# Node update of a graph layer: VectorE's sums one unit further ahead, slice weights folded in the first units, residual in three pieces

## The chip, the cores and the metric

The kernel runs on 1 core of one Trainium2 chip. The metric is the device time of one execution in microseconds, the median of several runs.

## The reference

One layer over a graph of 6250 nodes (256 features each) and 100,000 edges. `xn` is the row-wise layer norm of `x`.

```
x = x + gnn(xn, edges) + mix(xn)          # gnn: messages, then the node update below
x = x + ffn(layernorm(x))                 # ffn: slice attention over 8 heads of 64 slices

# the node update, inside gnn
agg  = segment_sum(msg, dst, 6250)
h    = silu(agg @ Wu1 + bu1) @ Wu2 + bu2
bn   = gamma * (h - mean(h, axis=0)) * rsqrt(var(h, axis=0) + 1e-5) + beta
return xn + bn

# the start of ffn; x_mid is (x @ W_x + b_x), cut into 8 heads
slice_weights = softmax((x_mid @ W_slice + b_slice) / clip(temperature, 0.1, 5))
```

The mean and variance of `h` run over all nodes, so no node can be normalised before `h` of the last node exists. `W_x @ W_slice / temp` and its bias don't depend on the nodes: they can be multiplied into one matrix beforehand ("folded").

## The kernel before

The kernel is a row of stages, each a block in which every engine has a program of its own and in which engines meet only at semaphores: `opening`, `messages_and_attention` (most of the time), `update_nodes`, `slice_tokens`, `slice_attention`, `slice_output`. Every engine runs its own instructions strictly in the order written, so an instruction that waits holds up all behind it on its engine. The change is inside `update_nodes`.

**The units.** The nodes are 49 tiles of 128. `update_nodes` walks over them in 13 units: 2 tiles, then eleven units of 4 tiles, then 3. The aggregated messages come in as 4 partial tables in DRAM. For each unit u:

- SyncE (SP) loads the unit's rows of the four tables, 512 KB each for a unit of 4 tiles, into one of 4 buffer sets (`load`). Sets 0 and 1 are the tensors `part`; sets 2 and 3 are lent from `g.res`, rows of tiles 0 to 15 and 16 to 31, which are free until the residual is loaded. In the trace the tile is therefore called `part` or `res`. A set is loaded again once its unit has been summed (`agg_ready`) and transposed (`turned`).
- GpSimd (POOL) adds tables 2 and 3 (`late_sums`, line 1521). VectorE (DVE) adds tables 0 and 1 (line 1544), then GpSimd's sum (line 1547); both are `gather_sums`. Both operands of all these additions lie in SBUF.
- TensorE (PE) transposes the sum (`turn_sums`, line 1383), ScalarE (ACT) rounds it to `agg_high` (`high_sums`, line 1467), VectorE subtracts to get `agg_low` (`low_sums`, line 1553, one operand in PSUM).
- TensorE multiplies by Wu1 in three high/low products (`hidden`, line 1395, 12 matmuls). ScalarE applies silu (line 1474) and rounds (line 1481), GpSimd subtracts (`low_hidden`, line 1526, both operands in SBUF). TensorE multiplies by Wu2 (`nodes`, line 1409, 12 matmuls), ScalarE copies out to `hT` (`copy_h`, line 1486), VectorE takes the statistics (`node_stats`, line 1558, one operand).

TensorE's order is `hidden(u)`, `turn_sums(u+1)`, `nodes(u-1)`. ScalarE's is silu and round of u, `high_sums(u+1)`, `copy_h(u-1)`. GpSimd's is `low_hidden(u)`, `late_sums(u+2)`. VectorE's is

```
for u in range(UNITS):
    if u + 1 < UNITS:
        gather_sums(u + 1)
        low_sums(u + 1)
    if u:
        for f in range(CB):
            node_stats(u - 1, f)
```

so that on VectorE `node_stats(u-1)` stands between `low_sums(u+1)` and `gather_sums(u+2)`.

**The end of the stage.** After the last unit VectorE joins the statistics (line 1611), ScalarE takes the square root (line 1504), and VectorE runs `fold_slices` (lines 1564 to 1582), for which TensorE has multiplied the slice weights (lines 1428, 1431, 1435) after its last `nodes`. Only then come the reciprocal (line 1616) and three small operations that give scale and shift. Then the back part: ScalarE normalises `hT` unit by unit (line 1509), TensorE transposes it back (line 1445), VectorE adds the residual (line 1629) and takes row statistics (line 1633). The residual is loaded in two pieces (lines 1371 and 1372) once the last unit is summed and transposed, since half of the lent sets is in use until then.

Of the kernel before, what the change touches and what calls it, by code (L numbers as in the profile page):

```python
# [43 lines left out]
TABLES = 4  # L44
# [1207 lines left out]
SETS = 4  # L1252

# [17 lines left out]
def update_nodes(nc, sem, sb, g):  # L1271
# [61 lines left out]
    FOLD_BIAS = 7  # L1333
    heads = lambda ap: ap.rearrange("p (h n) -> p h n", h=FH)
# [17 lines left out]
    with nc.Block() as block:  # L1352
        @block.sync
        def _(sp):
# [13 lines left out]
            sp.wait_ge(agg_ready, UNITS)  # L1368
            sp.wait_ge(turned, PAIRS_BEFORE[UNITS])
            half = NT // 2  # L1370
            sp.dma_start(g.res[:, 0:half, :], split_rows(g.res_dram, 0, half)).then_inc(res_in, 16)
            sp.dma_start(g.res[:, half:NT, :], split_rows(g.res_dram, half, NT - half)).then_inc(res_in, 16)

        @block.tensor
        def _(pe):
# [36 lines left out]

            turn_sums(0)
# [10 lines left out]
            pe.wait_ge(turn_low, PAIRS_BEFORE[UNITS])  # L1424
            pe.wait_ge(hid_ready, CB * UNITS)
            for b in range(CB):
                for h in range(FH):
                    nc.tensor.matmul(g.ps[b][:, ds(h * FG, FG)], wx_t[:, h, ds(b * P, P)], w_slice[:],
                                     start=True, stop=True)
            for h in range(FH):  # L1430
                mm = nc.tensor.matmul(g.ps[2][0:1, ds(h * FG, FG)], b_x[:, h:h + 1], w_slice[:], start=True, stop=True)
            mm.then_inc(folded, 1)

            pe.wait_ge(fold, FOLD_BIAS)
            nc.tensor.matmul(g.ps[3][0:BIAS_ROWS, :], ends[:], bias[:], start=True, stop=True).then_inc(folded, 1)

# [78 lines left out]
        def _(pool):  # L1515
# [13 lines left out]
            late_sums(0)  # L1529
            late_sums(1)  # L1530
            for u in range(UNITS):
                for f in range(CB):
                    low_hidden(u, f)
                if u + 2 < UNITS:
                    late_sums(u + 2)

        @block.vector
        def _(dve):
# [21 lines left out]
            def fold_slices():  # L1560

                dve.wait_ge(fold, 5)
                dve.wait_ge(folded, 1)
                V.tensor_tensor(heads(bias[:]), heads(g.ps[2][0:1, :]),
                                b_slice[:].unsqueeze(1).to_broadcast([1, FH, FG]), ALU.add).then_inc(fold, 1)
                dve.wait_ge(fold, 6)
                V.tensor_tensor(heads(bias[:]), heads(bias[:]), wide(inv_temp[0:1, :], 1),
                                ALU.mult).then_inc(fold, 1)
                for b in range(CB):
                    V.tensor_tensor(heads(w_logit[:, b, :]), heads(g.ps[b][:]), wide(inv_temp[:], P),  # L1570
                                    ALU.mult).then_inc(logit_w, 1)
                dve.wait_ge(logit_w, CB)
# [3 lines left out]
                dve.wait_ge(folded, 2)  # L1576
                V.tensor_copy(spread, g.ps[3][0:BIAS_ROWS, :]).then_inc(fold, 1)
                dve.wait_ge(fold, 8)
                V.tensor_copy(g.logit_bias[:], spread).then_inc(fold, 1)
                dve.wait_ge(fold, 9)  # L1580
# [615 lines left out]
```

## Time and profile before

| | us |
|---|---|
| median of 3 runs | 2219.74 |
| lowest, highest run | 2217.71, 2225.6 |
| the profiled execution: its own time | 2217.5 |
| the profiled execution: span of its instructions | 2215.7 |
| `update_nodes` within it, first load to last row statistic | 1703.1 to 1876.8 |

Times are microseconds from the start of the span unless marked ns. In the rows DVE is VectorE, ACT ScalarE, POOL GpSimd, SP SyncE, PE TensorE's matmuls and PEld its weight loads. L1544 is line 1544 of the kernel. A row of the timeline gives start, duration, engine, line, operation, output and inputs, and in brackets how long the engine had been idle before and which instruction ended that. In the table of windows the columns are the stretch, its length, for PE, PEld, DVE, ACT and POOL the busy time with the count of instructions, then PEclk, the DMA share and GB/s. PEclk is the mean clock that TensorE was granted, 1.00 for 2.4 GHz and 0.50 for 1.2 GHz; DMA is the mean busy share of the DMA engines.

### The profile page before, as it was taken

To read this page: it belongs to the slowest core of one execution; us is meant where nothing else is said; L and a number is where in the kernel's file an instruction comes from. 1 tells how busy PE (TensorE), PEld (TensorE's weight loads), DVE (VectorE), ACT (ScalarE), POOL (GpSimd) and SP (SyncE) were. 2 spreads that over 40 slices of the span, in tenths; PEclk is the share of its full clock that TensorE was granted. 3 is DMA by queue.
4 is the path that set the end of the run, shared out by engine and by line. 5 is a ranking of instruction groups with operands and counts; after the bars stand their busy time and mean duration, and the time that the engine had idled before them with its cause. 6 is when DMAs were issued, how large, how long until landed. Compare 5 with 4: busy or idle time off the path is not lost. (4 is left out here: it accounts for less than half of the span.)

```text
span 2215.7 us, 38972 instructions
## 1 busy us (share of the span) xinstructions
PE 1914.7 (86%) x10218; PEld 1580.6 (71%) x10218; DVE 1531.5 (69%) x3525; ACT 1306.3 (59%) x2330; POOL 1437.9 (65%) x989
## 2 busy tenths in 40 slices
PE   3687999999889988998899989998990785999878
PEld 2466788777777777877787777877880574788678
DVE  6654777777767767776777676767771568999645
ACT  2333776776676657765776676667660463666423
POOL 2121888888888888888888888888885550455300
PEclk9898999999999999999999999999995895999979
DMA  8756888988888889878888888898886951000002
GB/s 280 278 223 204 159 156 153 188 152 147 146 179 156 152 156 172 156 138 161 168 156 155 176 154 156 142 181 156 148 132 112 329 161 54 1 0 0 20 20 97
DMA packets 288441, 325.45 MB, mean 147 GB/s; under 512 B 29575, under 2 KB 251178, under 8 KB 288146
## 3 DMA queue, kind: packets, MB, share of 16 engines
q0 software_dynamic: 112896, 102.81, 37.8%
q1 hardware_dynamic: 169568, 216.13, 30.8%
q10 hardware_dynamic: 5746, 3.90, 0.7%
q8 instruction: 88, 1.44, 0.3%
q14 instruction: 143, 1.17, 0.2%
HBM read 167.64 MB, written 154.97 MB: 146 GB/s over the span
## 5 line engine op out<-in xcount | busy, mean ns | idle before, releaser
L903 POOL DMA_INDIRECT sums<-summed,out_idx x784 | 1236.1, 1577 | 295.1 <-issue 209.5
L957 PE MATMUL bank<-wf,hidT 128*128 128x256 f32 x3136 | 798.3, 383 | 0.0
L957 PEld LDWEIGHTS bank<-wf,hidT 128*128 128x128 f32 x3136 | 544.5, 192 | 54.1
L1048 ACT ACTIVATE hidT<-bank,bf 128x512 f32<-128x512 f32 x392 | 269.8, 688 | 263.0 <-PE bank L935 216.6
L1143 DVE TENSOR_TENSOR msg_low<-msg,msg_high 128x512 fp32r<-128x512 f32 x392 | 272.4, 695 | 180.0 <-ACT msg_high L1068 133.5
L1174 DVE TENSOR_TENSOR msg<-bank,gathered 128x512 f32<-128x512 f32 x392 | 269.4, 687 | 111.3 <-PE bank L957 83.5
L1068 ACT ACTIVATE msg_high<-msg 128x512 fp32r<-128x512 f32 x392 | 247.2, 631 | 93.2 <-DVE msg L1174 83.6
L955 PE MATMUL bank<-gnn_bf_halves,ones 128*128 128x256 f32 x784 | 297.1, 379 | 0.0
L1056 ACT ACTIVATE summed<-pair 128x516 f32<-128x516 f32 x392 | 230.2, 587 | 59.2 <-DMA sums<-summed,out_idx 56.1
L1075 ACT ACTIVATE gathered<-bank 128x512 f32<-128x512 f32 x392 | 231.9, 592 | 51.0 <-issue 22.6
L945 PE MATMUL bank<-window,spread 128*128 128x256 f32 x784 | 194.1, 329 | 66.7 <-DVE spread L1138 38.9
L935 PE MATMUL bank<-attr_parts,wf_parts 128*128 128x512 f32 x392 | 224.4, 572 | 26.2 <-DVE attr_parts L1128 22.5
L969 PE MATMUL pair<-msg_high,same 128*128 128x258 f32 x784 | 209.3, 288 | 21.8 <-ACT summed L1056 14.4
L945 PEld LDWEIGHTS bank<-window,spread 128*128 128x128 f32 x784 | 124.6, 191 | 129.5 <-issue 86.1
L969 PE MATMUL pair<-msg_low,same 128*128 128x258 f32 x784 | 206.3, 284 | 0.0
L1138 DVE TENSOR_TENSOR spread<-id_row,half_f 128x256 fp32r<-128x256 uint8 x392 | 165.4, 422 | 26.5 <-issue 17.6
L969 PEld LDWEIGHTS pair<-msg_high,same 128*128 128x128 f32 x784 | 149.5, 191 | 45.2 <-issue 21.0
L1153 DVE TENSOR_TENSOR same<-id_row,src_f 128x256 fp32r<-128x256 int16 x392 | 162.7, 416 | 0.0
L969 PEld LDWEIGHTS pair<-msg_low,same 128*128 128x128 f32 x784 | 148.8, 190 | 15.3
L955 PEld LDWEIGHTS bank<-gnn_bf_halves,ones 128*128 128x128 f32 x784 | 150.2, 192 | 10.7
L1163 DVE SCALAR_TENSOR_TENSOR redirect<-summed,first_limit,to_trash 128x2 f32<-128x2 f32 x392 | 85.5, 218 | 57.7 <-ACT summed L1056 45.7
L935 PEld LDWEIGHTS bank<-attr_parts,wf_parts 128*128 128x128 f32 x392 | 75.2, 192 | 63.3 <-issue 38.5
(329 smaller groups left out, 2818.6 us busy)
## 6 DMA issues: line engine op xcount, KB each, us to landing
window<-xn_halves SPq DMA_DIRECT2D x392, 128.0 KB
sums<-gate SPq DMA_DIRECT2D x32, 800.0 KB, 10.0
id_row<-id_rows SPq DMA_DIRECT2D x98, 256.0 KB
attr<-attr_rows SPq DMA_DIRECT2D x98, 256.0 KB
xn_halves<-xn_halves SPq DMA_DIRECT2D x7, 1792.0 KB, 6.6
id_row<-id_rows SPq DMA_DIRECT2D x98, 128.0 KB
sums<-summed,out_idx POOLq DMA_INDIRECT x784
res<-sums SPq DMA_DIRECT2D x24, 512.0 KB, 8.4
```

Of the source, the lines that this page charges most:

```text
L903: nc.gpsimd.indirect_dma_start(g.sums_dram[k], bass.IndirectOffsetOnAxis(ap=out_idx[:, ET * c + t:ET * c + t + 1], axis=0), summed[c % 2][ ...
L935: T.matmul(hps[:], g.wf1_parts[:, h, ds(f * P, P)], attr_parts[:, p, :], start=True, stop=True).then_inc(hid_made, 1)
L945: mm = T.matmul(gps[:, ds(t * C, C)], spread[:, j % 2, ds(t * P, P)], window[:, j, :], start=True, stop=True)
L955: T.matmul(out, g.ones2[:], g.bf2[:], start=True, stop=False)
L957: mm = T.matmul(out, hidT[:, j // 2, f, ds((2 * (j % 2) + t) * P, P)], g.wf2[:, f, :], start=False, stop=f == CB - 1)
L969: mm = T.matmul(sps[:, t, 0:XW], same[:, p, 2 * j + t, :], half[:, j % 2, t, :], start=k == 0, stop=k == 1)
L1048: A.activation(hidT[:, h, f, :], hps[:], ACT.Silu, bias=g.bf1[:, f:f + 1]).then_inc(hid_ready, 1)
L1056: A.activation(summed[p][:, ds(2 * j, 2), :], sps[:, :, 0:XW], ACT.Copy).then_inc(sum_ready, 1)
L1068: A.activation(msg_high[:, j % 2, :, 0:C], msg[:, j % 2, :, :], ACT.Copy).then_inc(high_ready, 1)
L1075: A.activation(gathered[:, j, :, :], gps[:].rearrange("p (t c) -> p t c", c=C), ACT.Copy).then_inc(gath_copied, 1)
L1143: V.tensor_tensor(msg_low[:, j % 2, :, 0:C], msg[:, j % 2, :, :], msg_high[:, j % 2, :, 0:C].bitcast(F32), ALU.subtract).then_inc(low_read ...
L1174: V.tensor_tensor(msg[:, j % 2, :, :], fps[j % 2][:].rearrange("p (t c) -> p t c", c=C), gathered[:, j, :, :], ALU.mult).then_inc(msg_read ...
```

## The change

Four edits, all in `update_nodes`.

1. On VectorE `gather_sums` runs one unit further ahead, and before `node_stats`. Its order is now `low_sums(u+1)`, `gather_sums(u+2)`, `node_stats(u-1)`.
2. GpSimd's `late_sums` runs 3 units ahead instead of 2.
3. The fold of the slice weights moves from the end to the first units. TensorE runs `fold_weights` after `hidden(0)` and `fold_ends` in unit 2; VectorE runs `fold_bias` before unit 1's `low_sums`, `fold_logits`, `round_logits` and `spread_bias` in units 0, 1 and 2. Banks 5 to 7 and the last columns of `hT`, unused that early, hold the intermediate results.
4. The residual comes in three pieces: tiles 32 to 48 behind the last table load, tiles 0 to 15 once unit 10 has been summed and transposed, tiles 16 to 31 once unit 11 has.

```diff
+AHEAD = 3
-    flat = [part[p][:, 0, :, :].rearrange("p t c -> p (t c)") for p in range(2)]
-    w_logit = flat[0].rearrange("p (b n) -> p b n", b=CB)
-    spread = flat[1][0:BIAS_ROWS, 0:HG]
+    w_logit = hT[:, :, ds(NPAD - HG, HG)]
+    spread = hT[0:BIAS_ROWS, 0, ds(NPAD - 2 * HG, HG)]
+    FOLDED_BANKS, BIAS_BANK, ENDS_BANK = g.ps[6:8], g.ps[5], g.ps[6]
+    LENT_SETS = {2: 0, 3: 1}
+    LENT = len(LENT_SETS) * TABLES * UT
+    LENT_SPLIT = TABLES * UT
...
         def _(sp):
...
-            sp.wait_ge(agg_ready, UNITS)
-            sp.wait_ge(turned, PAIRS_BEFORE[UNITS])
-            half = NT // 2
-            sp.dma_start(g.res[:, 0:half, :], split_rows(g.res_dram, 0, half)).then_inc(res_in, 16)
-            sp.dma_start(g.res[:, half:NT, :], split_rows(g.res_dram, half, NT - half)).then_inc(res_in, 16)
+            sp.dma_start(g.res[:, LENT:NT, :], split_rows(g.res_dram, LENT, NT - LENT)).then_inc(res_in, 16)
+            for u, landed in ((UNITS - 3, res_in), (UNITS - 2, slice_in)):
+                at = LENT_SETS[u % SETS] * TABLES * UT
+                sp.wait_ge(agg_ready, u + 1)
+                sp.wait_ge(turned, PAIRS_BEFORE[u + 1])
+                sp.dma_start(g.res[:, at:at + TABLES * UT, :], split_rows(g.res_dram, at, TABLES * UT))\
+                  .then_inc(landed, 16)
...
         def _(pe):
...
             def nodes(u):
...
+                if u == 0:
+                    pe.wait_ge(fold, FOLD_BIAS - 1)
...
             for u in range(UNITS):
                 hidden(u)
+                if u == 0:
+                    fold_weights()
                 if u + 1 < UNITS:
                     turn_sums(u + 1)
+                if u == 2:
+                    fold_ends()
                 if u:
                     nodes(u - 1)
             nodes(UNITS - 1)
-            pe.wait_ge(slice_in, 80)
...
-            mm.then_inc(folded, 1)
-
-            pe.wait_ge(fold, FOLD_BIAS)
...
+            pe.wait_ge(fold, FOLD_STEPS)
...
         def _(pool):
...
-            late_sums(0)
-            late_sums(1)
+            for u in range(AHEAD):
+                late_sums(u)
             for u in range(UNITS):
                 for f in range(CB):
                     low_hidden(u, f)
-                if u + 2 < UNITS:
-                    late_sums(u + 2)
+                if u + AHEAD < UNITS:
+                    late_sums(u + AHEAD)
...
         def _(dve):
...
+            gather_sums(1)
+            fold_bias()
             for u in range(UNITS):
                 if u + 1 < UNITS:
-                    gather_sums(u + 1)
                     low_sums(u + 1)
+                if u + 2 < UNITS:
+                    gather_sums(u + 2)
+                if u == 0:
+                    fold_logits()
+                if u == 1:
+                    round_logits()
+                if u == 2:
+                    spread_bias()
                 if u:
                     for f in range(CB):
                         node_stats(u - 1, f)
...
             V.tensor_scalar(sd[:], mv[:, :, 1], EPS, None, ALU.add).then_inc(chain, 1)
-            fold_slices()
             dve.wait_ge(chain, 4)
...
                     dve.wait_ge(back_made, n + 1)
+                    if LENT_SPLIT in tiles:
+                        dve.wait_ge(slice_in, 96)
```

`fold_weights` holds the matmuls of lines 1431 and 1428, in that order, `fold_ends` that of line 1435. `fold_bias`, `fold_logits`, `round_logits` and `spread_bias` hold the instructions of `fold_slices`, lines 1564 to 1582, in their old order.

## Rows read from the trace of the kernel before

**Rows 1.** Busy time by windows: units 1-3, units 4-11, end chain, back part.

```profile
1731.38:1757.92 26.54, 22.15 (x96) 17.80 (x97) 15.27 (x17) 13.18 (x23) 13.64 (x9) 0.86 1.10 348
1757.92:1819.17 61.25, 52.39 (x255) 41.83 (x254) 39.41 (x49) 38.72 (x64) 37.62 (x24) 1.00 0.52 164
...
1828.70:1840.76 12.06, 5.61 (x35) 3.37 (x34) 6.87 (x15) 2.57 (x5) 0.00 (x0) 0.60 0.70 225
1840.76:1876.80 36.04, 21.93 (x94) 15.42 (x94) 34.72 (x82) 15.68 (x24) 0.00 (x0) 0.59 0.00 0
```

**Rows 2.** Timeline of TensorE, one unit: hidden, transposes, nodes, next hidden.

```profile
1796.66 0.39 PE L1395 MATMUL bank<-agg_high,wu1h 128*128 128x512 f32 x1
...
1800.72 1.09 PE L1383 MATMUL bank<-ident,res 128*128 128x128 f32 x8 [1.17 <-DVE res L1547]
1801.57 0.48 PE L1409 MATMUL pair<-hid_high,wu2h 128*128 128x512 f32 x1
...
1804.42 0.39 PE L1395 MATMUL bank<-agg_high,wu1h 128*128 128x512 f32 x1
```

**Rows 3.** Timeline of VectorE, the same unit and the next sums.

```profile
1802.10 1.29 DVE L1553 TENSOR_TENSOR agg_low<-bank,agg_high 128x512 fp32r<-128x512 f32 x2 [1.44 <-ACT agg_high L1467]
...
1805.35 0.69 DVE L1558 BATCH_NORM_STATS2 bn_raw<-hT 128x6 f32<-128x512 f32 x1 [0.69 <-ACT hT L1486]
1805.96 1.21 DVE L1544 TENSOR_TENSOR res<-res 128x1024 f32<-128x1024 f32 x1
1807.20 1.23 DVE L1547 TENSOR_TENSOR res<-res 128x1024 f32<-128x1024 f32 x1
```

**Rows 4.** Timeline of ScalarE, the same unit.

```profile
1801.47 1.09 ACT L1467 ACTIVATE agg_high<-bank 128x512 fp32r<-128x512 f32 x2 [0.16 <-PE bank L1383]
...
1804.62 0.69 ACT L1486 ACTIVATE hT<-pair,bu 128x512 f32<-128x512 f32 x1 [0.69 <-PE pair L1409]
```

**Rows 5.** Timeline of GpSimd, unit 2's sum, and the same unit as above.

```profile
1728.83 2.35 POOL L1521 TENSOR_TENSOR res<-res 128x1024 f32<-128x1024 f32 x1 [0.30 <-DMA res<-sums]
...
1800.87 2.53 POOL L1526 TENSOR_TENSOR hid_low<-hidT_u,hid_high 128x512 fp32r<-128x512 f32 x2 [2.84 <-ACT hid_high L1481]
1803.36 2.39 POOL L1521 TENSOR_TENSOR res<-res 128x1024 f32<-128x1024 f32 x1
```

**Rows 6.** Timeline, unit 3: a sum on GpSimd and one on VectorE meet.

```profile
1740.11 2.40 POOL L1521 TENSOR_TENSOR res<-res 128x1024 f32<-128x1024 f32 x1
1740.46 3.13 DVE L1544 TENSOR_TENSOR res<-res 128x1024 f32<-128x1024 f32 x1
```

**Rows 7.** Timeline, the end chain: fold matmuls, root, reciprocal, first residual add.

```profile
1826.36 3.78 PE L1428 MATMUL bank<-w_slice,wx_t 64*128 64x64 f32 x32
...
1828.76 0.20 ACT L1504 ACTIVATE bn_sd<-bn_sd 128x2 f32<-128x2 f32 x1 [0.42 <-DVE bn_sd L1613]
1830.07 1.05 PE L1431 MATMUL bank<-w_slice,b_x 64*1 64x64 f32 x16
...
1832.68 2.07 PE L1435 MATMUL bank<-slice_bias,slice_bias_ends 1*128 1x512 f32 x2 [1.56 <-DVE slice_bias L1567]
...
1837.60 0.17 DVE L1616 RECIPROCAL bn_sd<-bn_sd 128x2 f32<-128x2 f32 x1
...
1840.76 0.69 DVE L1629 TENSOR_TENSOR res<-pair,res 128x512 f32<-128x512 f32 x1 [2.40 <-PE pair L1445]
```

**Rows 8.** The DMA issue of the residual's second half, on SP's timeline.

```profile
1817.09 5.10 SPq L1372 DMA_DIRECT2D res<-res_rows  x1
```

**Rows 9.** DMA issues by size: the last number is us from issue to landing.

```profile
res<-res_rows SPq DMA_DIRECT2D x1, 3200.0 KB, 21.2
```

**Rows 10.** Timeline, the opening: slice weights landed, and unit 1's first transposes.

```profile
1720.92 0.17 DVE L1597 TENSOR_SCALAR temp<-temp 128x8 f32<-128x8 f32 x1 [2.35 <-DMA temp<-w_ffn_temperature]
...
1728.00 1.97 PE L1383 MATMUL bank<-ident,part 128*128 128x128 f32 x8 [6.38 <-DVE part L1547]
```

**Rows 11.** Busy time by windows: just behind unit 0's hidden.

```profile
1721.70:1725.50 3.80, 0.00 (x0) 0.00 (x0) 1.23 (x1) 1.04 (x3) 2.70 (x1) 0.95 1.10 349
```

More of the change, by code:

```diff
@@ L1411, in nodes, with fold_weights, fold_ends @@
                     mm.then_inc(h_made, 1)
+            def fold_weights():
+                pe.wait_ge(slice_in, 80)
+                for h in range(FH):
+                    mm = nc.tensor.matmul(BIAS_BANK[0:1, ds(h * FG, FG)], b_x[:, h:h + 1], w_slice[:],
+                                          start=True, stop=True)
+                mm.then_inc(folded, 1)
+                for b in range(CB):
+                    for h in range(FH):
+                        mm = nc.tensor.matmul(FOLDED_BANKS[b][:, ds(h * FG, FG)], wx_t[:, h, ds(b * P, P)],
+                                              w_slice[:], start=True, stop=True)
+                mm.then_inc(folded, 1)
+            def fold_ends():
+                pe.wait_ge(fold, FOLD_BIAS)
+                pe.wait_ge(logit_w, CB)
+                nc.tensor.matmul(ENDS_BANK[0:BIAS_ROWS, :], ends[:], bias[:], start=True, stop=True)\
+                  .then_inc(folded, 1)
             turn_sums(0)
@@ L1421, in _ @@
             nodes(UNITS - 1)
-            pe.wait_ge(slice_in, 80)
[L1424 to L1431, printed above, removed]
-            mm.then_inc(folded, 1)
-            pe.wait_ge(fold, FOLD_BIAS)
-            nc.tensor.matmul(g.ps[3][0:BIAS_ROWS, :], ends[:], bias[:], start=True, stop=True).then_inc(folded, 1)
+            pe.wait_ge(fold, FOLD_STEPS)
             for u in range(UNITS):
@@ L1558, in node_stats, with fold_bias, fold_logits, round_logits @@
                 V.bn_stats(raw[:, f, u, :], hT[:, f, ds(UNIT_AT[u] * P, unit_nodes(u))]).then_inc(stats, 1)
[L1560 removed]
+            def fold_bias():
                 dve.wait_ge(fold, 5)
                 dve.wait_ge(folded, 1)
[L1564 removed]
+                V.tensor_tensor(heads(bias[:]), heads(BIAS_BANK[0:1, :]),
                                 b_slice[:].unsqueeze(1).to_broadcast([1, FH, FG]), ALU.add).then_inc(fold, 1)
[L1566 removed]
+                dve.wait_ge(fold, FOLD_BIAS - 1)
                 V.tensor_tensor(heads(bias[:]), heads(bias[:]), wide(inv_temp[0:1, :], 1),
                                 ALU.mult).then_inc(fold, 1)
+            def fold_logits():
+                dve.wait_ge(folded, 2)
                 for b in range(CB):
[L1570 removed]
+                    V.tensor_tensor(heads(w_logit[:, b, :]), heads(FOLDED_BANKS[b][:]), wide(inv_temp[:], P),
                                     ALU.mult).then_inc(logit_w, 1)
+            def round_logits():
                 dve.wait_ge(logit_w, CB)
@@ L1575, in fold_slices, with spread_bias @@
                 V.tensor_tensor(g.logit_low[:], w_logit, g.logit_high[:].bitcast(F32), ALU.subtract)
-                dve.wait_ge(folded, 2)
-                V.tensor_copy(spread, g.ps[3][0:BIAS_ROWS, :]).then_inc(fold, 1)
-                dve.wait_ge(fold, 8)
+            def spread_bias():
+                dve.wait_ge(folded, 3)
+                V.tensor_copy(spread, ENDS_BANK[0:BIAS_ROWS, :]).then_inc(fold, 1)
+                dve.wait_ge(fold, FOLD_BIAS + 1)
                 V.tensor_copy(g.logit_bias[:], spread).then_inc(fold, 1)
-                dve.wait_ge(fold, 9)
+                dve.wait_ge(fold, FOLD_STEPS)
                 low = slice(LOW_ROW, LOW_ROW + 1)
```

1 line of the change is left out of this document (added).

## The prediction

> **What bounds the kernel now.** I read the table of windows first, to see what each stretch of the stage is worth and who fills it, then the timelines of the engines over one unit, and last the timeline of the end. `update_nodes` is 174 us of the run and falls into four stretches [rows 1]. From `hidden(1)` to `hidden(4)` 26.54 us pass, with a granted clock of 0.86: part of it ran at 1.2 GHz. From `hidden(4)` to `hidden(12)` it is 61.25 us for eight units, 7.66 each, at full clock. Then an end chain, 12.06 us from the square root to the first residual add, in which TensorE and GpSimd are nearly idle. Then the back part, 36.04 us, in which VectorE is busy for 34.72: nothing of the change touches its work, so it only moves.
>
> In a full unit 7.76 us lie between two `hidden` (1796.66 to 1804.42) [rows 2]. TensorE is not the bound: it stands idle 1.17 us ahead of its transposes, for the sum. Followed back, the wait is a ring: transposes 0.85 (1800.72 to 1801.57) [rows 2], `nodes` 2.85 (1801.57 to 1804.42), then 0.20 until ScalarE's copy starts, 0.69 for the copy (from 1804.62) [rows 4], 0.65 until the statistics on it are out of VectorE's way (1805.31 to 1805.96) [rows 3], the two sums 2.47 (1805.96 to 1808.43) [rows 3], 0.05 to the next transposes. That adds to 7.76, the whole period. The statistics need `nodes`, the sums behind them don't; only VectorE's order ties them.
>
> **The end chain.** The root is ready at 1828.76 + 0.20 = 1828.96 and the reciprocal that needs it starts at 1837.60 [rows 7]. Between lie the fold's instructions: VectorE waits for the matmuls (3.78 and 1.05 us), then does its nine. Without them the reciprocal starts some 0.1 us behind the root, as the other steps of that chain follow each other. That removes 8.5 us, and the first residual add comes at 1832.3 instead of 1840.76.
>
> It needs the residual to be there. Before, the second half was issued at 1817.09 [rows 8] and landed 21.2 us later [rows 9], at 1838.3: left so, it would have given back 6.0 of the 8.5. Edit 4 removes that: the last piece waits only for the transposes of unit 11, some 15 us ahead of the end of the loop, and is 2 MB; at the 348 GB/s that the DMA engines moved when full [rows 1] it takes 6 us. The first piece joins SP's queue behind all table loads, so it delays none. Edit 4 costs nothing then, as long as the loop still covers it.
>
> **The steady units.** With the sums of u+2 issued ahead of the statistics the ring above is cut. What is late next? Three things stand close together. TensorE itself: 7.76 less the 1.17 of idling, 6.59 us. The chain that needs one `hidden` for the next: from `hidden` at 1796.66 through silu and rounding to the end of `agg_low` at 1803.39 [rows 3], less the 0.16 for which ScalarE waited for transposes [rows 4], 6.57. And the side-by-side work of VectorE and GpSimd.
>
> That third one is why I don't take 6.6. In unit 3 a sum on VectorE started at 1740.46 while one on GpSimd ran from 1740.11 to 1742.51; it lasted 3.13 us, against 1.21 alone, and ended 1.08 after GpSimd's did [rows 6, 3]. So these operations, with both operands in SBUF, exclude each other. `agg_low` with an operand in PSUM, and the statistics with one operand, overlap GpSimd's work without growing. Per unit GpSimd holds 2.53 + 2.39 = 4.92 [rows 5], VectorE 1.21 + 1.23 = 2.44: together 7.36. At present they hardly meet, because the sums start at 1805.96, just behind GpSimd's end at 1805.75. Moved ahead of the statistics, they start about where `late_sums` does, and the two collide in every unit. A handover hides a little (1.08 of 1.21), four of them at about 0.15 take 7.36 to 6.8. So the period has its bounds at 6.6 (no cost of collision) and 7.76 (all gain lost to it). I take 7.1 for full units: above 6.8, because the lock is idle while GpSimd waits for the rounding, and below 7.36, because VectorE's other 2.7 us of work don't need it. On eight units, the last one shorter, I count 0.62 each, 5.0 us; bounds 0 and 8 x 1.06 = 8.5.
>
> The Trainium skill ("SBUF — State Buffer", section Who interferes with whom) says that a VectorE instruction with two SBUF inputs contends with a GpSimd instruction that reads SBUF, and that whoever issues first holds the port for the whole instruction. The row of unit 3 agrees, 3.13 us for 1.21. By that rule taken strictly the period would not fall under the 7.36 of the plain sum, and the eight units would give 2.4 us instead of 5.0.
>
> **The first units.** From `hidden(1)` to `hidden(4)` three units take 26.54 us, 3.3 more than three steady ones: low clock, and the blocked sum of 3.13. At the new period three units are 21.3. Against it stands what the fold adds there: on TensorE one matmul of 2.07 us, measured at 1.2 GHz [rows 7], about half of it if the clock is up; on VectorE 3.7 us of rounding and spreading in units 1 and 2, ahead of the next `agg_low`, and VectorE was busy only 15.27 of 26.54 [rows 1]. I let 1.0 us of both reach the path: 22.3, a gain of 4.2. Bounds: 0, if the clock stays low, and 6.7, if the period is 6.6 and the fold is hidden.
>
> **The opening.** The matmuls of `fold_weights` fall behind `hidden(0)`, which ends at 1721.7; the slice weights had landed at 1720.9, and TensorE then idled 6.38 us to 1728.00 [rows 10]. They take 3.78 + 1.05 = 4.8 us at full clock, and the stretch behind `hidden(0)` was granted 0.95 [rows 11]: done at 1726.5, at no cost. At 1.2 GHz I bound them at twice that, 9.7, less the 6.38 of cover: 3.3 late. `fold_bias` on VectorE, 1.4 us, follows unit 1's sum and ends as `agg_high` of unit 1 does. The third `late_sums` on GpSimd, now ahead of `low_hidden(0)`, needs unit 2, which landed at 1728.8 [rows 5]; it ends at 1731.2, `low_hidden(0)` some 2.4 later, and `nodes(0)`, behind `hidden(1)`, asks for it only at about 1735. A unit's tables are 2.1 MB, 6.0 us at 348 GB/s: unit 3 at 1734.8, unit 4 at 1740.8, and so on. Sums at a period of 7.1 fall further behind these landings with each unit, so the DMA is not the bound, though by just 1.1 us a unit.
>
> **The sum.** 8.5 + 4.2 + 5.0 = 17.7 us. The profiled execution took 2217.5 us, the median of the runs is 2219.74, 2.2 above it and the lowest run 2217.71; I take the middle, 2218.6, and get 2200.9, as 2201.
>
> **The rivals.**
>
> *Collision eats the loop.* The idle wait for the sum goes, but VectorE blocked behind `late_sums` brings `agg_low` late instead; the period stays at 7.66 and the opening gives 2.0. Then 8.5 + 2.0 = 10.5: 2208. For it: the row of 3.13 and the 7.36. Against: VectorE waits 1.44 us ahead of `agg_low` at present [rows 3] and has room for one blocked sum.
>
> *TensorE-bound.* The engines fall into a phase in which they don't meet: period 6.6, 8.5 + 6.7 + 8.5 = 23.7, 2195. Against: the lock would have to be busy without a gap.
>
> *The opening pays back.* The fold's matmuls run at 1.2 GHz and `hidden(1)` is 3.3 late: 14.4 us, 2204. For it: the clock was at 0.50 again when the transposes came; against: the 0.95 just before.
>
> *Slower.* VectorE loses the lock ahead of each of its two sums, once to `late_sums` and once to both `low_hidden`: its own round is 1.29 + 2.39 + 1.21 + 2.53 + 1.23 + 1.38 = 10.0 us. Eight units then lose 18.7, the first three 3.5, the end gives 8.5: 13.7 slower, 2232. It decides from a period of about 9. Against it: in unit 3 VectorE got the lock as soon as the running GpSimd instruction ended.
>
> **Chances.** Forecast 0.50, collision 0.20, TensorE-bound 0.13, opening 0.14, slower 0.03. The range takes the two ends of the steady and first units: 2194 (all at 6.6, and the median at the lower side) to 2209 (the collision case). 0.5% of 2219.74 is 11.1 us, so faster is below 2208.6, about what a measurement of this kernel can tell from no change. Of the collision case 0.12 falls below and 0.08 within, and of the opening's 0.01 within: faster 0.88, same 0.09, slower 0.03.
>
> **What would show it.** The reciprocal directly behind the root, and the first residual add, with no wait for a DMA, some 3.4 us behind the root. No idle time of TensorE ahead of the transposes; in its place a small wait for `agg_low`. Means of lines 1544, 1547, 1521 and 1526 that grow, by a few tenths of a us and up to 2: the sum of the growths is the price of the collision. A period near 7.1. A period of 7.6 or more, a `hidden(1)` later than 1732, or a residual add that waits for its piece would each make the prediction wrong.

## The result, and the profile after

| | before | changed |
|---|---|---|
| median, us | 2220.25 (7 runs) | 2211.66 (7 runs) |
| lowest to highest | 2217.71 to 2225.6 | 2209.71 to 2215.68 |
| the profiled execution, own time / span | 2217.5 / 2215.7 | 2210.18 / 2208.4 |

The ratio is 0.9959, with a 95% interval from 0.9947 to 0.9972: faster, by 8.6 us, where 17.7 had been forecast. The measured time lies above the stated range.

The message stage ahead of `update_nodes` ends some microseconds earlier or later in each execution: in the profiles of this study `update_nodes` begins between 1702 and 1712 us. So the stage is read by itself here. This table holds the stretches of `update_nodes`, taken from the timelines of ScalarE and VectorE. S is VectorE's first instruction in the stage, s1, s4 and s12 are ScalarE's first silu of units 1, 4 and 12, A is the joining of the statistics, R the first residual add, E the start of the last reciprocal.

| execution | S to s1 | s1 to s4 | s4 to s12 | s12 to A | A to R | R to E | stage |
|---|---|---|---|---|---|---|---|
| before | 31.15 | 25.13 | 60.96 | 7.21 | 13.11 | 35.53 | 173.1 |
| before, again | 30.14 | 24.62 | 60.86 | 7.23 | 13.56 | 35.54 | 172.0 |
| changed | 30.50 | 26.91 | 58.52 | 7.24 | 4.56 | 35.53 | 163.3 |
| changed, again | 34.37 | 26.85 | 58.50 | 7.24 | 4.56 | 35.54 | 167.1 |

The end gives 8.55 to 9.0 us, as forecast. Units 4 to 11 give 2.4 instead of 5.0, the first units lose 1.8 to 2.2 instead of giving 4.2, and the opening is as before in one execution and 3 to 4 us longer in the other. Part of that last difference is no work of the change: the first silu of unit 0 comes 17.18 and 16.17 us after S in the two executions of before, 16.30 and 18.05 in the two of the changed kernel. Counted from that silu, the stage takes 155.9 and 155.8 us before, 147.0 and 149.0 changed.

The table of windows of the changed kernel, for the stretches of [rows 1]; the first two again go from `hidden(1)` to `hidden(4)` and on to `hidden(12)`:

```profile
1732.42:1760.60 28.18, 25.20 (x98) 18.98 (x98) 22.81 (x24) 12.97 (x23) 19.63 (x12) 0.79 1.10 348
1760.60:1819.45 58.85, 52.41 (x255) 41.83 (x255) 53.38 (x49) 38.19 (x64) 41.09 (x24) 1.00 0.82 266
1829.10:1832.62 3.52, 1.08 (x4) 0.71 (x4) 0.69 (x6) 2.63 (x6) 0.00 (x0) 0.54 0.00 0
1832.62:1868.65 36.03, 22.06 (x94) 15.52 (x94) 34.73 (x82) 15.62 (x24) 0.00 (x0) 0.59 0.00 0
```

In the second row VectorE is busy for 53.38 us against 39.41 before, with the same 49 instructions, and GpSimd for 41.09 against 37.62. Nothing was added there: the 14 and 3.5 us are time in which an instruction had begun and stood still. In the first row the clock is 0.79 instead of 0.86.

VectorE's timeline over one steady unit of the changed kernel (lines 1571, 1562, 1565 and 1576 are what 1553, 1544, 1547 and 1558 were), answering to [rows 3]:

```profile
1789.09 1.29 DVE L1571 TENSOR_TENSOR agg_low<-bank,agg_high 128x512 fp32r<-128x512 f32 x2 [0.35 <-ACT agg_high L1485]
1790.29 1.46 DVE L1562 TENSOR_TENSOR part<-part 128x1024 f32<-128x1024 f32 x1
1791.79 3.30 DVE L1565 TENSOR_TENSOR part<-part 128x1024 f32<-128x1024 f32 x1
1795.02 1.27 DVE L1576 BATCH_NORM_STATS2 bn_raw<-hT 128x6 f32<-128x512 f32 x2
1796.53 1.29 DVE L1571 TENSOR_TENSOR agg_low<-bank,agg_high 128x512 fp32r<-128x512 f32 x2 [0.24 <-ACT agg_high L1485]
```

and GpSimd's beside it, answering to [rows 5]:

```profile
1788.12 2.55 POOL L1544 TENSOR_TENSOR hid_low<-hidT_u,hid_high 128x512 fp32r<-128x512 f32 x2 [2.93 <-ACT hid_high L1499]
1790.63 3.38 POOL L1539 TENSOR_TENSOR res<-res 128x1024 f32<-128x1024 f32 x1
```

VectorE's second sum starts at 1791.79 and lasts 3.30 us instead of 1.23: GpSimd's sum, from 1790.63 to 1794.01, has the port. (It lasts 3.38 instead of 2.39 because VectorE's first sum had it until about 1791.7.) VectorE now goes from one `agg_low` to the next with hardly any idle time, 7.44 us: its own blocked work is the period. In some units it is the first sum that is blocked, behind GpSimd's sum, and the second that is free:

```profile
1782.81 3.47 DVE L1562 TENSOR_TENSOR part<-part 128x1024 f32<-128x1024 f32 x1
1786.31 1.23 DVE L1565 TENSOR_TENSOR part<-part 128x1024 f32<-128x1024 f32 x1
```

The period is therefore not one number. From silu to silu units 4 to 11 take 8.25, 7.11, 7.82, 7.36, 7.55, 7.37, 7.00 and 6.06 us, and in the second execution the same to 0.05; the first seven have a mean of 7.49. Where the text says 7.4, it means the shown unit.

The end, VectorE's timeline, answering to [rows 7]:

```profile
1829.40 0.17 DVE L1648 RECIPROCAL bn_sd<-bn_sd 128x2 f32<-128x2 f32 x1 [0.27 <-ACT bn_sd L1522]
...
1832.62 0.69 DVE L1663 TENSOR_TENSOR res<-pair,res 128x512 f32<-128x512 f32 x1 [2.46 <-PE pair L1463]
```

The reciprocal waits for the root alone, the residual add for transposes alone.

TensorE's timeline in units 1 and 2 (line 1437 is the bias matmul, formerly 1435):

```profile
1745.96 1.09 PE L1390 MATMUL bank<-ident,res 128*128 128x128 f32 x8 [1.63 <-DVE res L1565]
1746.98 1.62 PE L1437 MATMUL bank<-slice_bias,slice_bias_ends 1*128 1x512 f32 x2
1748.53 0.80 PE L1418 MATMUL pair<-hid_high,wu2h 128*128 128x512 f32 x1
1749.13 0.63 PE L1418 MATMUL pair<-hid_low,wu2h 128*128 128x512 f32 x1
```

and VectorE's:

```profile
1742.61 3.29 DVE L1565 TENSOR_TENSOR res<-res 128x1024 f32<-128x1024 f32 x1
1745.83 1.76 DVE L1595 CAST logit_high<-hT 128x1024 fp32r<-128x1024 f32 x1
1747.62 2.17 DVE L1597 TENSOR_TENSOR logit_low<-hT,logit_high 128x1024 fp32r<-128x1024 f32 x1
```

In the kernel before, the two instructions of the rounding stood in the end chain, with no GpSimd instruction beside them:

```profile
1833.86 0.70 DVE L1573 CAST logit_high<-part 128x1024 fp32r<-128x1024 f32 x1
1834.59 1.22 DVE L1575 TENSOR_TENSOR logit_low<-part,logit_high 128x1024 fp32r<-128x1024 f32 x1
```

Unit 3's sum is blocked to 3.29 us, TensorE idles 1.63 us for it, does 1.55 us of fold ahead of `nodes(1)`, and then runs `nodes(1)` with 0.63 us per matmul, at 1.2 GHz (0.39 at 2.4).

### The profile page after: what moved, and what is told of

Read it like the earlier page. It is cut to its first block and busy times, and to the rows that moved or that the text cites. A ratio compares the mean times of both kernels' runs of the same rounds, so it can differ in the third digit from the quotient of the medians.

```text
span 2208.4 us, 38977 instructions
## 1 busy us (share of the span) xinstructions
PE 1923.6 (87%) x10218; PEld 1586.1 (72%) x10218; DVE 1548.5 (70%) x3525; ACT 1306.1 (59%) x2330; POOL 1447.2 (66%) x989
## 5 line engine op out<-in xcount | busy, mean ns | idle before, releaser
L969 PEld LDWEIGHTS pair<-msg_high,same 128*128 128x128 f32 x784 | 149.7, 191 | 41.6 <-issue 16.4
```

The lines of the kernel that those rows point to most:

```text
L969: mm = T.matmul(sps[:, t, 0:XW], same[:, p, 2 * j + t, :], half[:, j % 2, t, :], start=k == 0, stop=k == 1)
```

## The experiments

Each ratio is to the kernel before, run on the same chip. The stage times stand in one table behind the experiments.

**E1. Fold and residual alone.**

```diff
-AHEAD = 3
+AHEAD = 2
...
             for u in range(UNITS):
                 if u + 1 < UNITS:
+                    if u:
+                        gather_sums(u + 1)
                     low_sums(u + 1)
-                if u + 2 < UNITS:
-                    gather_sums(u + 2)
```

> Edits 3 and 4 alone (fold in the first units, residual in three pieces); the order of the sums on VectorE and GpSimd is that of before. Theory P (collision): VectorE's sums moved ahead of the statistics collide with GpSimd's sums and give nearly nothing net, so the two other edits carry the whole gain: end chain 8.5 us shorter, units 4 to 11 at the old period of 7.75, first three units up to 1.5 us longer for the fold's work on VectorE and TensorE; in all 7 to 8.5 us faster than before, ratio 0.9962 to 0.9968. Theory F (the fold costs the gain): the fold's instructions in units 1 and 2 are what lengthened the first units by 1.8 us and more; then this kernel is only 4 to 6 us faster, ratio 0.9973 to 0.9982.

Ratio 1.0006 (0.9991 to 1.002): no gain at all, though the end is 8.6 us shorter. Both expectations missed, theory F by less. It is all lost before unit 4: S to s1 takes 33.92, s1 to s4 32.09. TensorE's timeline:

```profile
1754.52 1.97 PE L1390 MATMUL bank<-ident,res 128*128 128x128 f32 x8 [5.92 <-DVE res L1565]
1756.42 2.07 PE L1437 MATMUL bank<-slice_bias,slice_bias_ends 1*128 1x512 f32 x2
```

and VectorE's ahead of it:

```profile
1745.44 0.90 DVE L1595 CAST logit_high<-hT 128x1024 fp32r<-128x1024 f32 x1
1746.37 3.31 DVE L1597 TENSOR_TENSOR logit_low<-hT,logit_high 128x1024 fp32r<-128x1024 f32 x1
```

In this order the rounding of the logits stands ahead of unit 3's sum. GpSimd blocks it (3.31 us for 1.22), TensorE idles 5.92 us, and runs the bias matmul and most of `nodes(1)` at 1.2 GHz. One unit takes 17.06 us. From unit 4 on the period is 7.74, as before.

**E2. The sums alone.**

```diff
-            late_sums(0)
-            late_sums(1)
+            for u in range(3):
+                late_sums(u)
...
-                if u + 2 < UNITS:
-                    late_sums(u + 2)
+                if u + 3 < UNITS:
+                    late_sums(u + 3)
...
+            gather_sums(1)
             for u in range(UNITS):
                 if u + 1 < UNITS:
-                    gather_sums(u + 1)
                     low_sums(u + 1)
+                if u + 2 < UNITS:
+                    gather_sums(u + 2)
```

> Edits 1 and 2 alone (VectorE's and GpSimd's sums one unit further ahead); fold and residual stay at the end. Theory P (collision): VectorE's second sum takes about 3.3 us in most units, the period is 7.5 instead of 7.75, 2 us over units 4 to 11, and the first units gain 0 to 2: 2 to 4 us faster, ratio 0.9982 to 0.9991. Theory F: without the fold in the way the edit gives what the prediction said of it, 9 us, ratio 0.996, with a period near 7.1.

Ratio 0.9973 (0.9953 to 0.9994), about 6 us; the stage is 167.2, shorter by 5 to 6. Units 4 to 11 give 3.3 to 3.4, the first units 0.4 to 0.9, the opening 0.6 to 1.6. From silu 1 to silu 12 the sums give 3.7 to 4.3 us, where the prediction's terms without the fold would be 10.2 (5.0, and 26.54 less 21.3). That is more than in the changed kernel, whose first units lose. The second sum is blocked to 3.3 us here too, as theory P had it, though the ratio lies between the two theories. The first units have a slow one here as well, without any fold: unit 3 takes 10.54 us, with TensorE idle for 2.35 us ahead of its transposes and the first matmuls of `nodes(2)` at 0.63 us each, so at 1.2 GHz.

**E3. GpSimd's sums left out.** VectorE adds table 2 alone and table 3 is not added, so the output isn't the reference's.

```diff
-            for u in range(AHEAD):
-                late_sums(u)
...
-                if u + AHEAD < UNITS:
-                    late_sums(u + AHEAD)
...
-                dve.wait_ge(late_ready, u + 1)
```

> The changed kernel with GpSimd's sums of tables 2 and 3 left out (VectorE adds table 2 alone, table 3 is not added), and the wait for them. Everything else as in the changed kernel, so GpSimd holds only 2.5 us per unit. Theory P: VectorE's sums take 1.2 us each again and the period falls to 6.6 to 6.8, TensorE or the chain through the rounding being the bound; 6 to 9 us faster than the changed kernel, ratio to before 0.992 to 0.9935. Rival D (the table loads, 6 us a unit, or the chain of VectorE's own work set the period): the period stays at 7.3 or more and the time within 2 us of the changed kernel.

Ratio 0.9925 (0.9902 to 0.9947). From unit 4 to unit 10 the period is 6.64 to 6.68, and s1 to s4 takes 21.42: theory P. TensorE has no idle time ahead of its transposes in these units. The table loads, which are unchanged, allow 6.65.

**E4. The residual loaded late.**

```diff
-            sp.dma_start(g.res[:, LENT:NT, :], split_rows(g.res_dram, LENT, NT - LENT)).then_inc(res_in, 16)
...
+            sp.wait_ge(agg_ready, UNITS)
+            sp.wait_ge(turned, PAIRS_BEFORE[UNITS])
+            half = NT // 2
+            sp.dma_start(g.res[:, 0:half, :], split_rows(g.res_dram, 0, half)).then_inc(res_in, 16)
+            sp.dma_start(g.res[:, half:NT, :], split_rows(g.res_dram, half, NT - half)).then_inc(res_in, 16)
...
-                    if LENT_SPLIT in tiles:
-                        dve.wait_ge(slice_in, 96)
```

> The changed kernel with the residual loaded as before, in two halves once the last unit is summed and transposed. If edit 4 carries most of the gain at the end: the first residual add waits for the second half, which lands about 21 us after its issue, 5 to 6 us later than in the changed kernel; ratio to before 0.998 to 0.999. If the residual is hidden anyway: within 1 us of the changed kernel, ratio 0.996.

Ratio 0.9992 (0.9977 to 1.0008). A to R takes 9.96 instead of 4.56, so edit 4 is worth 5.4 us, as the first of the two expectations had it. VectorE's timeline and the DMA issues:

```profile
1848.56 0.69 DVE L1659 TENSOR_TENSOR res<-pair,res 128x512 f32<-128x512 f32 x1 [7.87 <-DMA res<-res_rows]
```

```profile
res<-res_rows SPq DMA_DIRECT2D x1, 3200.0 KB, 20.7
```

**E5. The statistics between the two sums.**

```diff
                 if u + 2 < UNITS:
-                    gather_sums(u + 2)
+                    first_sum(u + 2)
...
                 if u:
                     for f in range(CB):
                         node_stats(u - 1, f)
+                if u + 2 < UNITS:
+                    second_sum(u + 2)
```

> The changed kernel with VectorE's statistics of u-1 put between its two sums of u+2 (first sum, both statistics, second sum); in units 0 to 2 the fold's instructions follow the second sum. If VectorE's blocked second sum sets the period (theory P): the 1.4 us of statistics now run while GpSimd holds the port, the period falls from 7.4 to 6.7 to 6.9, 4 to 6 us less on units 4 to 11; the stage 158 to 160 us against 163 to 166 of the changed kernel, ratio to before 0.993 to 0.995. If the sum of all exclusive work (4.92 + 2.44 = 7.36) is the bound whatever the order: period 7.3 or more, time as the changed kernel.

Ratio 0.9978 (0.9962 to 0.9994), period 8.15: worse than the old order. The first expectation missed; the second's "7.3 or more" is met in number only, since 8.15 is 0.8 above the sum of 7.36 that it went by. VectorE's timeline:

```profile
1791.95 3.19 DVE L1562 TENSOR_TENSOR part<-part 128x1024 f32<-128x1024 f32 x1
1795.06 1.27 DVE L1583 BATCH_NORM_STATS2 bn_raw<-hT 128x6 f32<-128x512 f32 x2
1796.26 1.20 DVE L1568 TENSOR_TENSOR part<-part 128x1024 f32<-128x1024 f32 x1
1798.90 1.29 DVE L1578 TENSOR_TENSOR agg_low<-bank,agg_high 128x512 fp32r<-128x512 f32 x2 [1.44 <-ACT agg_high L1485]
```

Now the first sum is the blocked one, and the statistics stand again ahead of something that the next transposes wait for. I had counted VectorE's round, 6 us, and forgotten the ring of the prediction: `agg_low`, blocked sum, statistics, second sum, transposes, rounding, `agg_low`, 8.16 in all.

**E6. VectorE's fold late.** TensorE's fold matmuls stay behind `hidden(0)`. VectorE's product and rounding move to its idle time in units 10 and 11, the spreading of the bias to the wait for the first back transposes.

```diff
-    w_logit = hT[:, :, ds(NPAD - HG, HG)]
-    spread = hT[0:BIAS_ROWS, 0, ds(NPAD - 2 * HG, HG)]
-    FOLDED_BANKS, BIAS_BANK, ENDS_BANK = g.ps[6:8], g.ps[5], g.ps[6]
+    flat = [part[1][:, k, :, :].rearrange("p t c -> p (t c)") for k in range(2)]
+    w_logit = flat[0].rearrange("p (b n) -> p b n", b=CB)
+    spread = flat[1][0:BIAS_ROWS, 0:HG]
+    FOLDED_BANKS, BIAS_BANK, ENDS_BANK = g.ps[6:8], g.ps[5], g.ps[2]
...
-                if u == 2:
-                    fold_ends()
...
             nodes(UNITS - 1)
+            fold_ends()
...
-                if u == 0:
-                    fold_logits()
-                if u == 1:
-                    round_logits()
-                if u == 2:
-                    spread_bias()
...
+                if u == UNITS - 3:
+                    fold_logits()
+                    high_logits()
+                if u == UNITS - 2:
+                    low_logits()
...
+            spread_bias()
             dve.wait_ge(res_in, 32)
```

> The changed kernel with VectorE's fold instructions taken out of units 0 to 2: product and rounding in VectorE's idle time of units 10 and 11, the bias's spreading while the first back transposes run, TensorE's bias matmul behind its last nodes. TensorE's other fold matmuls stay behind hidden(0). Theory F (VectorE's fold work in units 1 and 2 delays the next sum and lets TensorE idle and its clock fall): hidden(1) to hidden(4) falls from 26.9 to 24 or 25 us, as with the sums alone (24.2), the rest is unchanged, ratio to before 0.9945 to 0.9955. Rival: the 26.9 come from the collision of the sums and the low clock alone; then 26 to 27 and no change.

Ratio 0.9948 (0.9934 to 0.9961). s1 to s4 falls to 21.02, further than theory F had it, and, not expected, the later units fall too, to 54.65. The program of a steady unit is the changed kernel's, word for word; only the moment at which the engines come into it differs. VectorE's and GpSimd's timelines:

```profile
1790.86 1.30 DVE L1562 TENSOR_TENSOR res<-res 128x1024 f32<-128x1024 f32 x1
1792.20 2.20 DVE L1565 TENSOR_TENSOR res<-res 128x1024 f32<-128x1024 f32 x1
1794.32 1.27 DVE L1576 BATCH_NORM_STATS2 bn_raw<-hT 128x6 f32<-128x512 f32 x2
```

```profile
1789.79 3.52 POOL L1544 TENSOR_TENSOR hid_low<-hidT_u,hid_high 128x512 fp32r<-128x512 f32 x2
1793.27 3.37 POOL L1539 TENSOR_TENSOR res<-res 128x1024 f32<-128x1024 f32 x1
```

Here VectorE's first sum falls between the two instructions of `low_hidden`, and its second behind the second of them, ahead of GpSimd's whole sum. So it waits for an instruction of 1.25 us, not for one of 2.4: 2.20 instead of 3.30. GpSimd's two rows add to 6.89 us in a period of 6.82 (a row begins before the one ahead of it has quite ended): it has no gap. This execution was the fastest of its kernel's ten (2203.66, median 2209.19), so its stage of 152.2 overstates the usual gain. The timed intervals of E6 and of the changed kernel (0.9947 to 0.9972) overlap; the difference between the two is read from the profiles.

**E7. The fold's matmuls split.**

```diff
-                for b in range(CB):
-                    for h in range(FH):
+                fold_block(0)
...
+                if u == 1:
+                    fold_block(1)
...
-                if u == 0:
-                    fold_logits()
                 if u == 1:
+                    fold_logits()
                     round_logits()
```

> The changed kernel with the fold's matmuls split: the bias and the first half behind hidden(0), the second half behind nodes(0), and VectorE's product in unit 1 instead of unit 0. Theory O (at 1.2 GHz the matmuls take 8.8 us and outlast the 6.3 us gap behind hidden(0)): from the stage's start to the first silu of unit 1 it is 31 to 31.5 us in runs with the low clock, as in before, instead of 33.7; units 1 to 4 take 0.5 to 3 us more because VectorE has the whole fold in units 1 and 2. Rival: the delay is the wait for the slice weights' landing, and stays 33.7.

Ratio 0.9958 (0.9941 to 0.9974), as the changed kernel. S to s1 takes 30.14, but this execution had the higher clock there, so it doesn't tell the two apart (E8 does); s1 to s4 is 27.86, 1.0 longer.

**E8. E5, E6 and E7 together.**

> All three of these at once: statistics between the sums, VectorE's fold late, TensorE's fold matmuls split. If the three costs are separate, they add: opening 31.3, units 1 to 4 22 to 24, units 4 to 12 53 to 55, to the aggregate 7.2, to the first residual add 4.6, back part 35.5: stage 154 to 157 us against 173.1 of before, ratio to before 0.991 to 0.993, faster than the changed kernel by 6 to 10 us. If one bound lies behind another (the table loads at 6.0 us a unit above all): 160 or more.

Ratio 0.9962 (0.9942 to 0.9983), stage 158.2, units 4 to 12 in 58.00. They don't add: units 4 to 12 take 3.4 us more than in E6. The order of E5 is the likely reason; it wasn't taken out by itself.

This execution had the low clock in the opening, and so it settles E7's question. TensorE's timeline, the first half of the split matmuls:

```profile
1724.24 3.67 PE L1433 MATMUL bank<-w_slice,wx_t 64*128 64x64 f32 x16
```

Half of the matmuls take about half of the 7.08 us that all take at 1.2 GHz, and silu 0 to silu 1 is 14.06 us instead of 16.3: theory O. It is the length of the matmuls that delays unit 1, not the landing of the slice weights.

**E9. GpSimd's sums in halves.**

```diff
-                G.tensor_tensor(c, c, d, ALU.add).then_inc(late_ready, 1)
+                n = len(unit_tiles(u)) // 2
+                for a in (slice(0, n), slice(n, None)):
+                    G.tensor_tensor(c[:, a, :], c[:, a, :], d[:, a, :], ALU.add).then_inc(late_ready, 1)
...
-                dve.wait_ge(late_ready, u + 1)
+                dve.wait_ge(late_ready, 2 * (u + 1))
```

> The changed kernel with each of GpSimd's sums of tables 2 and 3 cut into two instructions of half the size; the same work, the same order. Theory G (VectorE is held up by the length of the one GpSimd instruction that runs when it asks, 2.4 us for a whole sum and 1.25 for a half or for one half of low_hidden; not by the total of the work): VectorE's second sum takes 2.2 us instead of 3.3, the period of units 4 to 11 falls from 7.4 to 6.8 or 6.9, units 4 to 12 take 54 to 56 us instead of 58.5; the stage 159 to 162 us, ratio to before 0.994 to 0.995. Rival S (the sum of all exclusive work, which is the same or a little more here, sets the period): 7.3 or more and 58 to 59 us.

Ratio 0.9937 (0.9912 to 0.9962). Units 4 to 12 take 54.64, the period is 6.95 to 7.15 in units 4 to 9, with the same work and order as the changed kernel: theory G. The timed intervals of the two overlap (four runs here); the gain of 3.9 us in these units is read from the profiles. VectorE's and GpSimd's timelines:

```profile
1791.29 1.60 DVE L1564 TENSOR_TENSOR part<-part 128x1024 f32<-128x1024 f32 x1
1792.92 2.19 DVE L1567 TENSOR_TENSOR part<-part 128x1024 f32<-128x1024 f32 x1
```

```profile
1791.77 4.49 POOL L1541 TENSOR_TENSOR part<-part 128x512 f32<-128x512 f32 x2
```

The first units are no better (28.04).

**E10. E6 and E9 together.**

> The kernel with VectorE's fold late (52.2 us less than 58.5 was not its aim, but its units 4 to 12 took 54.65) and in addition GpSimd's sums in halves. If the two are the same gain got twice over, the port being busy without a gap at 6.8 us a unit: units 4 to 12 54 to 55 us, stage 152 to 154, ratio 0.9935 to 0.995, no faster than with the late fold alone. If halves shorten the waits beyond that: period 6.65, 53 us, stage 150 to 151.

Ratio 0.9913 (0.9891 to 0.9935), the lowest of all, 19 us faster than before. Its units 4 to 12 take 55.23, no less than in E6 or E9 alone: the same gain, reached by two ways. It enters the steady units at another moment than E9 does (21.48 against 28.04 us from s1 to s4) and comes to the same period, 6.94 to 6.99 in units 4 to 9. So that period goes with the halved sums and not with a lucky entry, which could not be said from E9 alone.

The late fold has a price that E6 didn't show by itself: unit 11 takes 6.83 us from silu to silu here, and 6.85 in E6, against 6.04 in E9. VectorE's timeline of this kernel,

```profile
1810.37 1.71 DVE L1598 CAST logit_high<-part 128x1024 fp32r<-128x1024 f32 x1
1811.99 1.01 DVE L1573 TENSOR_TENSOR agg_low<-bank,agg_high 128x512 fp32r<-128x512 f32 x2
```

and of E9:

```profile
1824.59 1.02 DVE L1573 TENSOR_TENSOR agg_low<-bank,agg_high 128x512 fp32r<-128x512 f32 x2 [2.05 <-ACT agg_high L1485]
```

In E9 VectorE stands idle for 2.05 us and waits for ScalarE; here the cast, blocked to 1.71 us, keeps it until after ScalarE is ready, and `agg_low` of unit 12 is late by some 0.8 us.

Against E6 the intervals just touch, so whether the halves add anything to the late fold is open; against the changed kernel (0.9947 to 0.9972) it is faster.

**E11 and E12. The changed kernel and the one before, once more.**

> The changed kernel once more, for its stage times in another execution. Units 4 to 12 58.5 us again (the same pattern of collisions, which then is set by the program and not by chance); from the stage's start to the first silu of unit 1 either 30.5 us (fold matmuls at 2.4 GHz for most of it) or 33.7 (at 1.2 GHz).

> The kernel before once more. If the stage's time is a property of the program: 173 us from start to end of update_nodes, within 2 us, whatever the time of the whole run, whose spread of 10 us would then come from the message stage ahead of it.

2214.23 and 2222.13 us. The stretches stand at the top: those behind silu 1 repeat to 0.5 us, and from unit 2 on each single unit repeats to 0.1. The opening differs. TensorE's timeline of the changed kernel in its first execution:

```profile
1722.60 1.50 PE L1425 MATMUL pair<-w_slice,b_x 64*1 64x64 f32 x16 [0.17 <-DMA temp<-w_ffn_temperature]
1724.03 4.43 PE L1430 MATMUL bank<-w_slice,wx_t 64*128 64x64 f32 x32
1729.04 1.97 PE L1390 MATMUL bank<-ident,part 128*128 128x128 f32 x8 [0.58 <-DVE part L1565]
```

and in the second:

```profile
1722.81 1.86 PE L1425 MATMUL pair<-w_slice,b_x 64*1 64x64 f32 x16
1724.60 7.08 PE L1430 MATMUL bank<-w_slice,wx_t 64*128 64x64 f32 x32
1731.61 1.97 PE L1390 MATMUL bank<-ident,part 128*128 128x128 f32 x8
```

with the window that holds the second's matmuls:

```profile
1722.50:1731.60 9.10, 9.10 (x50) 8.55 (x49) 3.72 (x4) 1.08 (x3) 5.67 (x2) 0.50 1.10 349
```

At 1.2 GHz the fold takes 8.8 us and outlasts the gap of some 6.3; silu 0 to silu 1 then takes 16.32 instead of 14.20; the other 1.75 us by which this opening is longer lie ahead of silu 0. There VectorE's cast of Wu1, which waits for the small weights' loads, starts 11.68 us after S in the first execution and 13.43 in the second:

```profile
1716.57 0.43 DVE L1616 CAST wu1h<-wu 128x512 fp32r<-128x512 f32 x1 [0.65 <-DMA beta<-w_gnn_beta]
1717.01 0.43 DVE L1616 CAST wu1h<-wu 128x512 fp32r<-128x512 f32 x1 [2.13 <-DMA beta<-w_gnn_beta]
```

The two executions of before differ by 1.0 us in the same place. Of the nine profiles with the fold whole behind `hidden(0)`, six show the long opening (16.3 to 16.4 us from silu 0 to silu 1) and three the short one (13.7 to 14.4).

The stretches of the experiments; s12 to A takes 7.2 us in all of them, R to E 35.5 to 35.6:

| kernel | S to s1 | s1 to s4 | s4 to s12 | A to R | stage | ratio |
|---|---|---|---|---|---|---|
| E1 fold and residual alone | 33.92 | 32.09 | 60.89 | 4.54 | 174.2 | 1.0006 |
| E2 sums alone | 29.58 | 24.21 | 57.60 | 13.11 | 167.2 | 0.9973 |
| E3 no sums on GpSimd | 31.65 | 21.42 | 52.66 | 4.56 | 153.0 | 0.9925 |
| E4 late residual | 33.67 | 26.90 | 58.50 | 9.96 | 171.8 | 0.9992 |
| E5 statistics between | 29.49 | 27.96 | 62.85 | 4.57 | 167.6 | 0.9978 |
| E6 VectorE's fold late | 29.32 | 21.02 | 54.65 | 4.39 | 152.2 | 0.9948 |
| E7 fold split | 30.14 | 27.86 | 58.74 | 4.57 | 164.1 | 0.9958 |
| E8 E5 to E7 | 29.15 | 23.68 | 58.00 | 4.57 | 158.2 | 0.9962 |
| E9 halved sums | 33.67 | 28.04 | 54.64 | 4.56 | 163.7 | 0.9937 |
| E10 E6 and E9 | 31.86 | 21.48 | 55.23 | 4.57 | 155.9 | 0.9913 |

## Why the prediction was wrong

**The end chain, 8.5 us: right.** 8.55 between the two profiles, with the reciprocal 0.03 us behind the root's end and the first add 3.3 behind the root. Edit 4 was priced at 6.0 and measured 5.4 (E4).

**The step that failed: the first units, forecast at 4.2 us gained.** They lost 1.8 to 2.2. The step took three units at the new period and "let 1.0 us of both reach the path". From `hidden(2)` to `hidden(3)` the changed kernel needs 12.53 us (1741.29 to 1753.82) against 10.25. The transposes wait for a sum of 3.29 us, come only 0.3 earlier than before and last 0.17 longer; the bias matmul lies on the path with 1.55, since it stands ahead of `nodes(1)`; and `nodes(1)` runs wholly at 1.2 GHz, 5.29 us against 4.43 (1745.76 to 1750.19 before, where the clock rose after seven of the twelve matmuls), 0.86 more. That is the 2.28. So the step failed in two places: the three units never came to the new period, since the blocked sum keeps TensorE waiting there too, and the fold put more than 1.0 us on the path. Its own length was priced; what GpSimd does to it (1.76 for a cast of 0.70, 2.17 for 1.22) wasn't, and "the clock stays low" was bounded at a gain of 0, where it was a loss. E1 shows the fold's share in the old order, 7.0 us in these three units (32.09 against 25.13), E2 the sums alone, 24.21, so the fold costs 2.7 in the new order. In E6, without VectorE's fold and the bias matmul there, the same three units take 21.02. That is 3.2 less than E2 with no fold at all, because E6 has no slow unit: so the 5.9 us between the changed kernel and E6 are not the fold's work alone. How much of them is the matmul, how much the clock and how much the moment at which the two engines meet wasn't taken apart, and whether the fold's work itself kept the clock down isn't shown.

**The steady units, forecast at 5.0: the collision was foreseen, its size was not.** They gave 2.4, so the term was 2.6 too large; the first units' term was 6.0 too large. The collision was the bound, and the ring is cut where it is taken away: E3, without GpSimd's sums, runs at 6.65, where 6.59 had been worked out. The collision was taken as a sum of exclusive work with a little hidden at handovers, 6.8 to 7.36, and the middle was chosen. The measured mean of units 4 to 10, 7.49, is above both. What counts is the length of the one instruction that has the port when VectorE asks. E9 changes that length, with the same work and order, and the same seven units come to a mean of 6.94; E6 reaches 6.82 with whole sums, by falling into another phase. So the sum of the work, less the handovers, fits as the floor (6.8 was worked out, and GpSimd has no gap in E6), and the changed kernel lies above it because VectorE's four stretches, one of them blocked for 2.1 us, add to 7.4. The rival "collision eats the loop" was the nearest, in its number and in that VectorE is held behind `late_sums`; the period did fall, though, and the first units were worse than it had them.

The Trainium skill ("SBUF — State Buffer", Who interferes with whom) agrees on the mechanism: the second to ask stands still until the first has finished, 3.30 us for 1.23. The 2.4 us worked out from it in the prediction is what the eight units gave, but for another reason: the plain sum of 7.36 is no bound, since E6 ran at 6.82 and E9 at 6.96.

**The opening, forecast at 0: 0.2 or 2.35.** The argument went by the granted clock of 0.95 just behind `hidden(0)`. No matmul ran in that stretch (x0 in [rows 11]), and it was one execution: in the second one of the kernel before the same stretch was granted 0.50. With the fold there, its 32 long matmuls took 7.08 us in six of nine executions, which is the time at 0.50, so the rival "the opening pays back" is what usually happens, at 2.35 of its 3.3 us.

**The sum.** With the measured terms: 8.55 + 2.44 - 1.8 + 0.65 = 9.8 for the first pair of profiles, whose stages differ by 9.8. The 0.65 is no gain of the change: silu 0 came 0.88 earlier, by the landing of the small weights, and the fold took 0.23 back. With the long opening 173.1 - 167.1 = 6.0. The timed 8.6 (6 to 12 by its interval) lies between. E1 shows how they hang together: fold and residual without the new order of sums gain nothing.

**Fewer idle waits of TensorE** were forecast; they remain, 0.4 to 1.7 us per unit for the sum, since the sum of u+2 is still what the next transposes need.

## What to carry to other kernels

Before moving a VectorE operation with two SBUF operands beside GpSimd's work, look not only at the busy shares but at the longest single GpSimd instruction that it can meet: that is the wait, and cutting the instruction in two, at the same total, gave 4 us in the steady units here. Work taken off an end chain is free only where its new neighbours have slack in every engine that it uses and the clock holds; the first units of a pipeline, waiting for loads, look idle and aren't. Right at the end of the same loop this fold cost 0.8 us, with its cast held up by GpSimd (1.71 us in E10, 1.38 in E6); in E8, where the cast took 0.69 us, unit 11 lost nothing (6.07).

## What the runs showed of the hardware

- A cast on VectorE with one SBUF operand (128x1024, float32) is held up by GpSimd too: 1.76 us beside `low_hidden` against 0.70 alone. The statistics, also one operand, were never held up: two of 512 columns took 1.27 to 1.29 us wherever they stood.
- TensorE was busy for 9.10 of 9.10 us with matmuls of 64 columns and stayed at 1.2 GHz throughout, where `hidden(1)` behind it was raised to 2.4 GHz towards the end of its 12 matmuls (0.63 us each until then, 0.39 after). In the first execution the same 32 matmuls took 4.43 us instead of 7.08: the clock rose among them.
- The same steady loop ran at 6.8 us a unit in E6 and swung from 8.25 over 7.11 and 7.82 to 7.37 in the changed kernel, depending on how the engines entered it; with GpSimd's sums cut in halves it ran at 6.95 from two different entries. A second execution of a kernel repeated the pattern of the first unit by unit.
